# Gather passes of a graph network: a cap on row reads under way instead of a wait at each chunk's end

## What is computed

```
GAT layer:   e   = leaky_relu(left[src] + right[dst])          per head
             w   = exp(e - max of e over the edges of dst)
             out = sum over the edges of dst of w * h[src], / sum of w
plain layer: out = sum over the edges of dst of rows[src]       (256 or 64 channels)
```

## Time and profile before

| | us |
|---|---|
| median of the runs | 9782.79 |
| profiled execution, its own time | 9857.64 |
| span of the profile | 9855.8 |
| PE busy | 5330.1 (54%) |
| DVE busy | 3876.0 (39%) |
| ACT busy | 3294.9 (33%) |
| POOL busy | 4640.0 (47%) |

### The profile page before, as it was taken

The page is one execution under the profiler, slowest core; times in us unless marked ns, Lnnn a source line. Parts: engine busy times, 40 slices in busy tenths (PEclk is TensorE's granted clock), DMA queues, the critical chain, the costliest instruction groups (busy, mean ns, idle before and its releaser), DMA issues. The chain is left out here.

```text
span 9855.8 us, 99024 instructions
## 1 busy us (share of the span) xinstructions
PE 5330.1 (54%) x20456; PEld 3980.8 (40%) x20457; DVE 3876.0 (39%) x9122; ACT 3294.9 (33%) x7862; POOL 4640.0 (47%) x4854
## 2 busy tenths in 40 slices
PE   2279844555543444458933333455555455555496
PEld 1155543344433333345633333244444334443364
DVE  3643384555571000044430000354445544446354
ACT  0042203333324333334523333233333333334253
POOL 4021106555525666532226666465654665664421
PEclk9669957777766777768955555577677676766598
DMA  1134313333323333222121111233332233332323
GB/s 47 70 116 182 147 18 97 90 88 87 89 64 91 92 91 92 80 87 64 58 69 23 23 23 23 63 91 84 90 87 80 83 91 87 87 88 65 104 63 119
DMA packets 433080, 786.36 MB, mean 80 GB/s; under 512 B 135112, under 2 KB 286506, under 8 KB 426034
## 3 DMA queue, kind: packets, MB, share of 16 engines
q0 software_dynamic: 208304, 507.09, 18.7%
q1 hardware_dynamic: 208950, 185.38, 6.4%
q10 hardware_dynamic: 15436, 90.13, 2.2%
HBM read 600.84 MB, written 187.29 MB: 80 GB/s over the span
## 5 line engine op out<-in xcount | busy, mean ns | idle before, releaser
L700 POOL DMA_INDIRECT g_rows<-table,src_idx x2352 | 2230.3, 948 | 1474.4 <-issue 701.8
L973 PE MATMUL g_p_win<-g_rows,g_hot 128*128 128x264 f32 (+1 forms) x4704 | 1529.2, 484 | 38.4 <-issue 31.5
L973 PEld LDWEIGHTS g_p_win<-g_rows,g_hot 128*128 128x128 f32 x4704 | 1087.7, 242 | 294.9 <-issue 65.5
L864 ACT ACTIVATE g_hot<-iota,near 128x128 f32<-128x128 f32 x2352 | 720.9, 387 | 996.2 <-DMA f_own<-table 435.2
L700 POOL DMA_INDIRECT g2p_rows<-rows,src_idx x784 | 749.4, 956 | 370.4 <-issue 228.5
L700 POOL DMA_INDIRECT gcnp_rows<-table,src_idx x784 | 739.6, 943 | 380.4 <-issue 227.7
L780 DVE TENSOR_TENSOR g_rows<-g_rows,g_p_w 128x1792 f32<-128x1792 f32 x336 | 679.1, 2021 | 73.7 <-issue 44.5
L2311 POOL DMA_INDIRECT back<-e_y,e_idx x210 | 205.2, 977 | 704.5 <-DVE e_idx L2402 545.7
L986 PE MATMUL g_p_f<-ones 1*128 1x4 f32 (+1 forms) x336 | 82.9, 315 | 753.0 <-ACT g_fold L889 282.6
L787 DVE TENSOR_TENSOR agg<-agg,g2p_p_out 128x256 f32 x112 | 42.2, 418 | 1113.1 <-PE g2p_p_out L935 417.6
L787 DVE TENSOR_TENSOR agg<-agg,gcnp_p_out 128x64 f32 x112 | 20.3, 221 | 1129.1 <-PE gcnp_p_out L935 660.2
(11 more groups left out here) (724 smaller groups left out, 10916.3 us busy)
## 6 DMA issues: line engine op xcount, KB each, us to landing
g_rows<-table,src_idx POOLq DMA_INDIRECT x2352
expert_rows<-e_zero ACTq DMA_DIRECT2D x28, 1332.5 KB
c_row<-back SPq DMA_DIRECT2D x35, 896.0 KB, 7.4
e_xin<-expert_rows SPq DMA_DIRECT2D x210, 130.0 KB
expert_rows<-e_zero ACTq DMA_DIRECT2D x13, 970.0 KB
back<-agg ACTq DMA_DIRECT2D x7, 1792.0 KB, 35.0
g2p_rows<-rows,src_idx POOLq DMA_INDIRECT x784
gcnp_rows<-table,src_idx POOLq DMA_INDIRECT x784
```

The costliest lines, as they stand in the source:

```text
L700: gp.indirect_dma_start(rows[:, s, j, 0:width + H], None, table, bass.IndirectOffsetOnAxis(g.src_idx[:, at:at + 1], 0)).then_inc(got[s], 16)
L864: last = nc.scalar.activation(hot[:, j, :], g.iota[:, :], ACT.Square, scale=-1.0, bias=g.near[:, bass.ds(c * J + j, 1)])
L973: last = nc.tensor.matmul(p_win[:, 0:W], hot[:, j, :], rows[:, s, j, :], start=(j == 0), stop=(j == J - 1))
```

## The change

GpSimd no longer waits at a chunk's end. The reads of a pass are numbered `at` = 14 c + j, and four semaphores `got` are used in turn, one read each. Before read `at` GpSimd waits for the landing of read `at` - 3. When that was the last read of a chunk, it increments a new semaphore, `landed`, by one. DVE (attention passes) and PE (plain passes) wait for `landed` instead of `got[s]`. The wait for `used` before a chunk stays. It holds in all five passes.

```diff
--- before.py
+++ after.py
@@ -92,6 +92,11 @@
         _, loaded = nc.values_load_multi_w_load_instructions(values, engines=(engine,), min_val=0, max_val=most,
                                                              skip_runtime_bounds_check_because="the program has made them itself, in this range")
     return loaded
+
+
+def landing(i):
+
+    return 16 * (i // (UNDER_WAY + 1) + 1)
 
 
 class Store:
@@ -337,6 +342,7 @@
     return g
 
 R = 4
+UNDER_WAY = 3
 
 
 class Norms:
@@ -632,7 +638,8 @@
             ph.sem(n) for n in ("seq", "setup_v", "squared", "halves", "used", "copied", "placed", "shifted", "added"))
         more_near_ready, more_parts, more_used, more_copied, more_shifted, more_added = (
             ph.sem(n) for n in ("more_near_ready", "more_parts", "more_used", "more_copied", "more_shifted", "more_added"))
-        got = [ph.sem(f"got{s}") for s in range(R)]
+        got = [ph.sem(f"got{s}") for s in range(UNDER_WAY + 1)]
+        landed = ph.sem("landed")
         if H:
             inj = ph.sb("inj", [P, R, J, Q])
             reset = ph.sb("reset", [Q, R, 2, P])
@@ -691,15 +698,22 @@
             @block.gpsimd
             def _(gp):
                 nc.gpsimd.iota(base_i[:, :], [[P, NT + 1]], base=0, channel_multiplier=0).then_inc(seq, 1)
+                def until_landed(read):
+                    gp.wait_ge(got[read % len(got)], landing(read))
                 for c in range(NC):
                     s = c % R
                     if c >= R:
                         gp.wait_ge(used, 2 * (c - R) + 4)
                     for j in range(J):
                         at = c * J + j
-                        gp.indirect_dma_start(rows[:, s, j, 0:width + H], None, table, bass.IndirectOffsetOnAxis(g.src_idx[:, at:at + 1], 0)).then_inc(got[s], 16)
-                    if H:
-                        gp.wait_ge(got[s], 16 * J * (c // R + 1))
+                        if at >= UNDER_WAY:
+                            until_landed(at - UNDER_WAY)
+                            if (at - UNDER_WAY) % J == J - 1:
+                                gp.sem_inc(landed, 1)
+                        gp.indirect_dma_start(rows[:, s, j, 0:width + H], None, table, bass.IndirectOffsetOnAxis(g.src_idx[:, at:at + 1], 0)).then_inc(got[at % len(got)], 16)
+                for read in range(NC * J - UNDER_WAY, NC * J):
+                    until_landed(read)
+                gp.sem_inc(landed, 1)
 
             @block.vector
             def _(dv):
@@ -733,7 +747,7 @@
                     def start():
                         dv.wait_ge(side[s], c_uses(c, s, 32))
                         do("sides", V.tensor_copy(v, inj[:, s, :, :].rearrange("p j q -> p q j")))
-                        dv.wait_ge(got[s], c_uses(c, s, 16 * J))
+                        dv.wait_ge(landed, c + 1)
                         do("left", V.tensor_tensor(v[:, H:Q, :], left, v[:, H:Q, :], ALU.max))
                         dv.wait_ge(spread, 2 * c + 2)
                         do("forward", V.tensor_tensor_scan(a[:, :, :].rearrange("p q j -> p (q j)"), resets_f[:, :, :].rearrange("p q j -> p (q j)"), flat_v, -BIG, ALU.add, ALU.max))
@@ -987,7 +1001,7 @@
                         nc.tensor.matmul(p_f[:, 0:H], moved[0:1, s % 2, 0:P], minus[0:1, :], start=False, stop=False)
                         nc.tensor.matmul(p_f[:, 0:H], moved[0:1, s % 2, 0:P], fold[0:1, :], start=False, stop=True).then_inc(factor, 1)
                     else:
-                        pe.wait_ge(got[s], c_uses(c, s, 16 * J))
+                        pe.wait_ge(landed, c + 1)
                     t(0)
                     if not first_of(c):
                         shift_before(c, s)
```

## The result

The changed kernel takes 9873.72 us, the median of four runs (9854.93 to 9874.31). The kernel before, run beside it, takes 9787.45 us (four runs). The ratio is 1.008, interval 1.0061 to 1.010: slower by 86 us (a small change, but clear of the noise), against 109 forecast. Two later sets of runs give 1.0117 (1.0096 to 1.0139) and 1.0073 (1.0044 to 1.0101).

A forecast was written before the change was run, and what follows sets the result against it. PE, DVE and ACT in turn were taken to bound the attention passes, themselves bounded by PE's completions arriving late while reads stream. Terms +60 + 31 + 18 = +109 us on the median 9782.8 gave 9892 us, 8-in-10 range 9420 to 9990.

The forecast's parts named there:

- The cap at 0: Each read waits for the read three before; already satisfied when reached, taken as 0, at most 0.7 us a read.
- The end wait ends last at 9 boundaries only: Attention passes, chunks 1 to 3: removing the chunk-end wait saves 1.8 us each, 16 us; elsewhere `used` is later.
- there I take 0: Attention boundaries that wait for `used`: removing the landing wait gains 0; bounds 0 and the whole 1.6 us.
- Start of a pass, +60: Attention passes, first four chunks in one stream: `used` comes later, 0 to 26 us a pass, 20 taken, 60 for three.
- Slack spent early, +31: Attention passes after the start: without the early lead long stops mix in at once, 15 us in g1, 8 each elsewhere.
- Two waits at a first read in the plain passes, +18: Plain passes, a chunk's first read: two waits add 0.49 us at each `used` stop, 0 to 35 us, 18 taken.
- The reading of the lateness: PE's completions reach other engines late while reads stream, and arrive when GpSimd has been still some 2 to 3 us.
- The landing wait as the real stop: Rival: the 117 short attention stops are the landing's and shrink to 0.30 us; 398 us faster, 9385; chance 0.07.
- The pacing rival: Rival: the cap slows every read to 1.43 us, PE's results flow, stops go; 347 us less, 9436; chance 0.22.
- The fourth rival: Longer streams hurt throughout attention passes: one long stop more in five boundaries, 172 us on top, 10064; chance 0.06.

The follow-up runs named there:

- late set: A set of runs in which the unchanged kernel, run beside the others, takes 9613 to 9796 us; three sets were of this kind.
- prompt set: A set of runs in which the unchanged kernel, run beside the others, takes 8890 to 8897 us; two sets were of this kind.

## Why the prediction was right, and where it wasn't

The sign was right, and so was the place in the main: the attention passes. That the size came out near (86 us against 109) is luck. The sum was 60 + 31 + 18. Of these the first and the last measured nothing, the middle one about half, and most of the loss (58 of 71 us in the gaps of the late set) lies at chunks 13 to 55, where the forecast had put nothing. Its own signs say the same: it expected the fifth chunk 90 to 106 us after the first, `g1` near 1290 us and later stops as before; the trace has 79.1 us, 1277 us and more long stops later on.

- **The cap at 0: right.** The wait is satisfied when it is reached, 0.014 us a read in the prompt set. In the late set the reads inside chunks are 46 us further apart in sum than without the cap (13 us over the pace without it, 59 with it), and the time isn't higher for it: the stops take it in. With two under way it would have bound.
- **The end wait ends last at 9 boundaries only: right for a late set.** At the 156 others `used` came 2.64 us or more after the last read's end, later than the landing at 146 of the 149 that the record has. In the prompt sets the landing ended the stop at all 165. But "there I take 0" had a second part that failed: the wait that hardly ever ended last still cost 0.5 us after `used` had come, and 0.2 us at the read behind it. Taking it out gave GpSimd an earlier start at every stop, which the sum did not have.
- **Start of a pass, +60: wrong, about 0.** The stop at chunk 4 came, 8.95 us long. The step that failed was to take it that the chain moves little until the stop, and to add its remaining 26 us. In the changed kernel, while the first stream ran:

```profile
1593.05 3.47 PE L987 MATMUL g_p_win<-g_rows,g_hot 128*128 128x272 f32 x14
...
1613.37 2.15 ACT L878 ACTIVATE g_hot<-iota,near 128x128 f32<-128x128 f32 x7 [24.32 <-DMA r_gb<-in_L_ffn_gate_b_dram]
...
1616.93 0.28 DVE L774 TENSOR_TENSOR g_p_v<-bwd_block,g_p_turn 128x112 f32<-128x112 bf16 x1 [24.15 <-DMA back<-e_y,e_idx]
...
1623.33 0.40 ACT L912 ACTIVATE g_win<-g_p_win 128x272 f32<-128x272 f32 x1 [1.53 <-DMA r_gb<-in_L_ffn_gate_b_dram]
```

  PE's sums of chunk 0 ended at 1596.52, 18.09 us before GpSimd's last read did (1614.61). Only the news of it was missing: the last increment of `used` is in the trace at 1623.30, and GpSimd goes on at 1623.56. The end, 79.1 us, is near the 80.1 of before, where the chain and three short stops took as long. The row that I had leaned on doesn't carry the term either: in `g2p` the copy that came 39 us late, at 3097.24, came while reads still streamed. The fifth chunk started there without a stop, 70.6 us after the first, and the stop of 10.84 us began at 3129.23 - 10.84 = 3118.39, a chunk later.
- **Slack spent early, +31: about half, and not the main loss.** The gaps at chunks 5 to 12 of the three passes grew by 16 us. What the forecast had wrong is that later stops stay as before: at chunks 13 to 55 there are 45 long gaps instead of 26, and 58 us.
- **Two waits at a first read in the plain passes, +18: wrong.** After a `used` stop in the changed kernel's g2p:

```profile
3204.12 0.38 ACT L912 ACTIVATE g2p_win<-g2p_p_win 128x256 f32<-128x256 f32 x1 [7.27 <-DMA f_own<-table]
3204.35 0.95 POOL L713 DMA_INDIRECT g2p_rows<-rows,src_idx  x1 [4.54 <-DMA f_own<-table]
```

  GpSimd starts 0.23 us after ACT, with two waits as with one. The 0.72 of the earlier trace rows belongs to a landing wait right before the wait for `used`, as the kernel with that wait in all passes shows, and not to the number of waits: here the order is the other way round. So the change took 0.49 us away at each stop of the attention passes where I had it add them in the plain ones. The passes confirm it: 1120 and 1116 us from first to last read, 1118 and 1119 before.
- **The reading of the lateness: right for late sets in the main.** Of the transposes that ended while reads streamed 154 of 195 were taken up late, of those that ended in a rest none of 33. "Arrive when GpSimd has been still for some 2 to 3 us" is too narrow: 63 of the 154 were taken up in mid-stream, and at chunk 4 above the increment took 8.7 us of rest. I also took the lateness for a property of the kernel, where it comes and goes between sets of runs with the kernel unchanged. The sentence of the Trainium skill that I set against it ("TensorE: Matmul & The Clock Gate", "The cost: per-tile semaphore tail", an estimate of 56 ns) has something near it where the sets are prompt: DVE starts 0.11 us after PE's end, its own start included.
- **The rivals.** The landing wait as the real stop had 0.07 for the set that was measured, and it was no part of it; in a prompt set it is the whole story, 302 us where I worked out 398. The pacing rival, with 0.22, needs 0.15 us a read from the cap; it has 0.014. The fourth rival, "longer streams hurt throughout", had 0.06 and is nearest to what the traces show: it worked out 33 more long stops all through the passes, and there are 23 more in the first pair of profiles and 26 more in the later set. It added 5.2 us for each; measured are 71 / 26 = 2.7.

No kernel here is the fastest in both kinds of set. In the prompt sets the one without wait and without cap is the fastest, 8587.81 us; in the late set of five the kernel before is.

## What to carry to other kernels

Before crediting a wait with the pause that it makes, look in the trace whether it ever ended last; here it did not at 146 of 149 boundaries, and its removal still cost 1%. A wait that is hardly ever the last may act through what comes behind it: compare how long the engine takes to start again, with it and without. Count stops of both sizes throughout a stage, not at its start. And when results are late, separate the work still to do from the news of work already done: only the first is added to a stop. A gain or loss near 1% that hangs on such a pause should be measured in several sets of runs: here the same edit is worth -3.4% in one kind and +1% in the other.

## What was not expected of the hardware

- The unchanged kernel takes 8890 to 8897 us in two sets and 9613 to 9796 in three. In the slower kind most results of PE that end while indirect reads stream reach DVE, ACT and GpSimd over 2 us late (154 of the 195 transposes counted, the longest 16 us; the sums of one plain chunk 39 us), and those that end while GpSimd rests come at once (the sums above 0.04 and 0.28 us later). It is the semaphore's increment itself that is late: for sums that ended at 1596.52 the trace has it at 1623.30, and ACT moves 0.03 us after it. In the faster kind none of the 177 transposes is late. What differs isn't known.
- When GpSimd waits for a landing and then at once for `used`, its next read comes 0.74 us after the increment that it waited for last, and 0.26 us when no landing wait stands right before. The landing had then been over for 1.5 us in the median.
- A wait on a semaphore that is already satisfied costs 0.014 us a read in GpSimd's stream of 1.25 us reads; three waits and an increment in a row, behind a chunk's last read, cost 0.6 us more than one wait.
